# Twelve one-hot buffers instead of two in the three SAGE passes of a four-layer graph network

## The reference

```python
deg = segment_sum(ones, edge_dst); inv_deg = where(deg > 0, 1 / max(deg, 1), 0)
def sage_conv(h, Ws, Wn, b):
    agg = segment_sum(h[edge_src], edge_dst)
    return h @ Ws + (agg * inv_deg) @ Wn + b
h = relu(sage_conv(x, Ws0, Wn0, b0))    # 128 -> 256
h = relu(sage_conv(h, Ws1, Wn1, b1))    # 256 -> 256
h = relu(sage_conv(h, Ws2, Wn2, b2))    # 256 -> 128
```

## Time and profile before

| | us |
|---|---|
| median of three runs | 5223.72 (5216.58 to 5224.33) |
| the profiled execution | 5251.98 |
| its span, first to last instruction | 5250.2 |
| PE, DVE, ACT, POOL busy in it | 3245.7, 2924.6, 2771.9, 2886.8 |

### The profile page before, as it was taken

How to read it: one execution, slowest core, us unless ns; L and a number is a source line. 1 busy time by engine, 2 the same in 40 slices (tenths; PEclk the granted TensorE clock), 3 DMA queues, 4 the chain that set the end, 5 groups by cost and what they waited for, 6 DMA issues and landing times.

```text
span 5250.2 us, 70737 instructions
## 1 busy us (share of the span) xinstructions
PE 3245.7 (62%) x16464; PEld 2658.9 (51%) x16465; DVE 2924.6 (56%) x6078; ACT 2771.9 (53%) x5854; POOL 2886.8 (55%) x2818
## 2 busy tenths in 40 slices
PE   4666667778885778884233364555723335777776
PEld 3555554667774667673223244444522324655554
DVE  3666674999997999996000001112100003999997
ACT  1656664777774777773333333333323332777773
POOL 3455521666663666663666625666166662666661
PEclk7888888665555665555555577777855555999996
DMA  4344421223332323321111122333111111333331
GB/s 141 110 118 120 121 75 35 76 76 78 78 78 52 76 76 77 76 75 42 43 46 47 45 64 76 91 91 89 30 44 46 47 45 39 97 98 96 96 98 30
DMA packets 326787, 385.94 MB, mean 74 GB/s; under 512 B 68200, under 2 KB 267806, under 8 KB 326270
## 3 DMA queue, kind: packets, MB, share of 16 engines
q0 software_dynamic: 102496, 236.78, 16.2%
q1 hardware_dynamic: 221910, 142.28, 9.8%
q10 hardware_dynamic: 2218, 4.94, 0.3%
HBM read 366.52 MB, written 17.21 MB: 73 GB/s over the span
## 4 chain that ended last, share of the span: by engine, by line
PE 31%; another core or an unknown queue 21%; DVE 17%; issue 15%; ACT 11%; DVEq 3%; DMA 1%; SPq 1%; ACTq 0%; POOL 0%
PE ps L737 6%; ACT onehot L882 5%; DVE big L1166 4%; PE ps L595 4%; PE ps L686 3%; PE ps L724 3%; ACT onehot L888 2%; DVE w_run L1344 2%; DVE y_sb L1166 2%; PE ps L716 2%; PE ps L790 2%; PE ps L785 2%; PE ps L519 2%; DVE big L1369 2%
## 5 line engine op out<-in xcount | busy, mean ns | idle before, releaser
L476 POOL DMA_INDIRECT big<-table_sage,src_block x1173 | 1110.3, 947 | 852.5 <-issue 331.6
L462 POOL DMA_INDIRECT rows<-table_gat,src_idx x832 | 924.4, 1111 | 746.3 <-PE ps L659 278.5
L882 ACT ACTIVATE onehot<-iota,dst_rel 128x128 f32<-128x128 f32 x1664 | 530.6, 390 | 1400.5 <-remote 1031.4
L785 PE MATMUL ps<-big,onehot 128*128 x2496 | 536.1, 385 | 789.9 <-ACT onehot L888 459.9
L785 PEld LDWEIGHTS ps<-big,onehot 128*128 128x128 f32 x2496 | 476.2, 283 | 847.2 <-issue 842.5
L737 PE MATMUL ps<-y_sb,onehot 128*128 128x136 f32 (+2 forms) x2496 | 664.2, 425 | 81.5 <-DVE big L1166 73.5
L1537 DVE TENSOR_TENSOR y_sb<-ps,inv_row 128x512 f32<-128x512 f32 (+1 forms) x14 | 8.0, 645 | 1226.3 <-PE ps L785 1226.3
L462 POOL DMA_INDIRECT rows<-table_pool,src_idx x416 | 480.5, 1155 | 311.6 <-PE ps L663 119.6
L1166 DVE TENSOR_TENSOR big<-big,ps 128x257 f32 (+3 forms) x1664 | 576.2, 346 | 87.1 <-PE ps L737 24.9
L737 PEld LDWEIGHTS ps<-y_sb,onehot 128*128 128x128 f32 x2496 | 516.3, 278 | 143.9 <-DVE big L1166 118.0
L476 POOL DMA_INDIRECT big<-table_mlp,src_block x391 | 370.8, 948 | 344.0 <-DVE ps L1186 186.4
(11 more groups left out here) (231 smaller groups left out, 5925.4 us busy)
## 6 DMA issues: line engine op xcount, KB each, us to landing
ea_sb<-in_ea_blocks SPq DMA_DIRECT2D x832, 64.0 KB
big<-neg_rows SPq DMA_DIRECT2D x312, 128.0 KB
ea_sb<-rel_rows SPq DMA_DIRECT2D x208, 128.0 KB
big<-table_sage,src_block POOLq DMA_INDIRECT x1173
rows<-table_gat,src_idx POOLq DMA_INDIRECT x832
rows<-table_pool,src_idx POOLq DMA_INDIRECT x416
big<-table_mlp,src_block POOLq DMA_INDIRECT x391
w_sb<-in_wpack ACTq DMA_DIRECT2D x1, 2374.0 KB
```

The lines of the kernel that those rows point to most:

```text
L462: pool.indirect_dma_start(to[g % 2][:, j, 0:ROW[k]], None, table[k], bass.IndirectOffsetOnAxis(src_idx[:, step:step + 1], 0)).then_inc(loa ...
L476: pool.indirect_dma_start(ring[:, (block + RING_FIRST[k]) % (n * G), :], None, table[k], bass.IndirectOffsetOnAxis(src_block[:, block:bloc ...
L785: mm = pe.matmul(to, onehot[:, b, j, :], row(j, 0), start=False, stop=False, skip_group_check=True)
L882: ins = act.activation(onehot[:, b, j, :], iota[:, 0:P], ACT.Square, bias=values[:, bass.ds(x * G + j, 1)], scale=-1.0)
```

## The change

The three SAGE passes take their one-hots from twelve buffers in turn. The two buffers of before are kept; the other ten are cut out of tiles that have other uses in other passes: `rows` (four groups), `ea_sb` (two), `w_run` and `s_run` (two each). ACT's group g now waits until group g - 12 is summed. Since `s_run` is scratch for the ring's slot numbers before sage0, ACT also waits for `slots_ready` once, at group 10 of sage0. PE reads the same buffers in the same turn. Sizes, operations and counts are as before, and so are the queues of POOL, SP and DVE; the ring's size and POOL's own wait are not touched. The mlp, attention and pool passes keep two buffers.

```diff
+        def groups_in(tile, first=0):
+            words = tile.rearrange("p g f -> p (g f)") if len(tile.shape) == 3 else tile
+            return [words[:, at:at + G * P].rearrange("p (g e) -> p g e", g=G) for at in range(first, words.shape[1], G * P)]
+
+        sage_onehots = [buf for tile in (onehot, rows, ea_sb) for b in range(2) for buf in groups_in(tile[:, b])]
+        sage_onehots += [buf for tile in (w_run, s_run) for b in range(2) for buf in groups_in(tile[:, b, :])]
+
+        def onehot_of(k, g):
+            if k in SAGE:
+                return sage_onehots[g % len(sage_onehots)]
+            return onehot[:, g % 2]
...
-                        mm = pe.matmul(to, onehot[:, b, j, :], row(j, 0), start=False, stop=False, skip_group_check=True)
+                        mm = pe.matmul(to, onehot_of(k, g)[:, j, :], row(j, 0), start=False, stop=False, skip_group_check=True)
...
-                            mm = pe.matmul(ps[:, 7, j * P:(j + 1) * P], onehot[:, b, j, :], row(j, 1), start=True, stop=True)
+                            mm = pe.matmul(ps[:, 7, j * P:(j + 1) * P], onehot_of(k, g)[:, j, :], row(j, 1),
+                                           start=True, stop=True)
...
             def mark_pass(k):
                 for g in range(NG):
-                    square_distances(k, g, g % 2, dst_rel)
-                    mark_edges(k, g, g % 2)
+                    n = len(sage_onehots)
+                    if k == "sage0" and g == n - 2:
+                        act.wait_ge(slots_ready, 2)
+                    if g >= n:
+                        act.wait_ge(summed, base[k] + g - n + 1)
+                    for j in range(G):
+                        ins = act.activation(onehot_of(k, g)[:, j, :], iota[:, 0:P], ACT.Square,
+                                             bias=dst_rel[:, g * G + j:g * G + j + 1], scale=-1.0)
+                    ins.then_inc(squares_ready, 1)
+                    act.wait_ge(squares_ready, SQUARED.index(k) * NG + g + 1)
+                    act.activation(onehot_of(k, g), onehot_of(k, g), ACT.Relu, bias=ones[:, 0:1], scale=-1.0)\
+                       .then_inc(onehot_ready, 1)
```

## The result

The changed kernel takes 5191.69 us, median of five runs (5188.38 to 5195.11), against 5223.72 us for the kernel before beside it (5216.58 to 5224.81): a ratio of 0.9947 (95% interval 0.9936 to 0.9957), so 32 us less. The prediction was 71 us less. The direction is right, and the time lies in the range, but less than half of the forecast gain came.

The account below looks back on a forecast made before the run. Gathers were taken as each SAGE pass's floor, with late PE completions keeping passes above it. Gains of 57 + 14 + 0 = 71 us from 5223.7 gave 5153, predicted as 5150 us, range 5060 to 5235.

Parts of the forecast that it names:

- floor of the gathers: POOL in each SAGE pass: 391 gathers back to back take 489 us, the least time of a pass.
- the loop: SAGE passes: a late completion on PE makes the one-hot late, then the sum, then the freeing of the ring.
- late completion: PE's finished sums reach the other engines late, 12 and 29 us at the start of sage2.
- (1): ACT's side: same squares and relus, ten more buffers and one new wait on `slots_ready`, costed at nothing.
- (2): POOL's waits on `summed` in sage0 and sage2 fall from 72.5 to 44 us each, together 57 us gained.
- PE then follows the landings: With one-hots ready, PE sums a group some 5 us after its last gather was issued.
- what would show it: Expected signs: POOL's waits about 50 us, 11 or 12 pauses, PE's sums released by gathers, tails 17 us, sage1 within 10.
- the last link: End of the chain of delays in the SAGE passes: a late sum frees the ring late, so POOL waits.
- (3): Ends of sage0 and sage2 after the last gather: 16.8 us in place of 21.6 and 26.2, gain 14 us.
- (4): sage1: ACT isn't in the loop that sets the pace, so 0 us, with -10 to +95 us as ends.
- PE is really late, or POOL's window alone decides: Rival on the SAGE passes, 17%: the lead wins nothing except the tails at most, 5224 to 5210 us.
- "slower" rival: Rival, 13%: completions handed out one at a time while POOL gathers, each open group costing another pause; 5377 us.

Follow-up runs that it names:

- chip 0: Both kernels run again unchanged on another chip than the first experiments': kernel before 4734.56 us, changed kernel 4731.28 us, ratio 0.9989.

## Why the prediction was partly right

**What bounds the kernel.** The floor of the gathers was read rightly: where nothing disturbs it, a pass is 487 us of gathers, for 489 worked out. That POOL waits on `summed` was right too. The first link of the loop, "late completion", was right in kind: the reports are late, on ACT as on PE. It was wrong in size and form: the prediction took it for a lateness of at most 29 us, and it grows with every group that PE finishes in such a stretch.

**(1), no cost.** Right: ACT's busy time in the passes is 198, 203 and 198 us (203, 205 and 202 before), and no wait for `slots_ready` shows.

**(2), 57 us: the step that failed.** It rested on two sentences: a late `summed` is late by up to 29 us, of which POOL's window bears about 20; and "PE then follows the landings", a group being summed 5 us after its last gather was issued, with another group or two reported while POOL gathers. The first half of what would show it did come: PE's sums are released by gathers in place of ACT. Here are PE's waits in sage0, of the kernel before and then of the changed one:

```profile
PE ps L785 <- ACT onehot L888: 268.0, 46, 20.3
PE ps L785 <- issue: 111.3, 27, 19.6
```

```profile
PE ps L797 <- DMA big<-table_sage,src_block: 199.9, 67, 4.4
PE ps L797 <- issue: 136.2, 92, 3.4
```

But with ACT out of the loop PE runs ahead of its reports. Groups 2 and 3 of sage0 are reported 35 and 48 us late in place of at most 29, and then PE needs 36 us for groups 6 and 7. POOL's six groups of window run out in 30 us. The rows of before held the sign: the report of group 3 of sage2 is 17 us later than that of group 2, for one more group, and 29 us was where two buffers stopped PE from piling up more. The "issue" waits of PE, 111 us before and 136 us after, were there too.

POOL's runs did grow, from at most 20 gathers to mostly 24 to 28, near the 28 to 32 forecast, but the pauses between them grew too, from 3 to 4 us to 4 to 5. The term came out as 9 + 9 = 18 us. The runs with PE late on purpose show the last link alone: where a sum comes late, ACT's lead does nothing for POOL's waits.

**(3), the tails, 14 us.** Right: 7.4 + 8.8 = 16 us, at 14.2 and 17.4 in place of 16.8. In the later runs (chip 0), where PE isn't behind at the last gather, the tails go from 16.8 and 17.7 to 13.2 and 15.9 us.

**(4), sage1, 0.** Right within its 10 us, 619 to 615 us, but not because nothing changed in the loop: POOL paused some 2.0 us after every 8 gathers before, and in the changed kernel some 2.45 us after every 12. What came of it is 6 us less of waits.

**The rivals.** "PE is really late, or POOL's window alone decides" had 17% and 5210 us at the most. Its second half is nearest to what came: the waits kept most of their sum, and the window decides; its time was too high by 18 us. Its first half the trace doesn't bear out, as four reports came within 2.0 us. I put against it that group 3 began while group 2 was unreported; with two buffers never more than two groups are in PE, too few to tell. The Trainium skill, "Perfetto Trace Analysis", Tensor Engine Instruction, says that a matmul's end in the trace is an estimate. No run here shows such an end to be wrong: the 104 reports of sage0 on the later chip agree with the ends within 0.02 us, and the late ones of the first runs come in bursts that point at the report.

The "slower" rival (13%, 5377 us) had the mechanism, reports handed out one at a time while POOL gathers, about every 20 us, with several groups open when POOL stops. It didn't have the price: it let each open group cost a pause of its own, but some 8 us after POOL stops the held reports come all at once.

**What stays open.** Why reports took 1.4 us an instruction in the first runs and not in those on three chips later, with the same program and, on chip 0, gathers of the same length and the same clock in the pass. As the first runs' chip isn't known, a difference of chips and a state that passed can't be told apart. No later run met these late reports, so that they depend on gathers without a pause is seen in the first traces only, and whether a wider ring or shorter runs of gathers would help against them wasn't tried.

## What to carry to other kernels

When reports come late, ask whether the lateness is fixed or grows: set the distance between two releases (17 to 22 us here) beside the distance between the pieces of work (5 us). If it grows, a longer lead only makes the backlog longer, and a window sized for one late report runs out. Several reports at one moment (here four groups in 2.0 us, work for 6.3) tell that the work was done and the reports were held. More buffers ahead of a late engine buy only its catching up and its tail; its consumer's window is what bears the lateness (twelve buffers: nothing of 227 us of waits; a ring twice as long: three quarters). Run the kernel before on a second chip, or at another time, ahead of tuning a wait that no instruction in the trace explains: here 489 us, and most of what the change was to cure, were not there.

## What the hardware showed

Unexpected were the reports at 1.40 us for each instruction on PE and ACT in the same stretch, with ACT's own squares (four in 1.26 us) and POOL's gathers (1.25 us apart before, in and after the stretch) undisturbed; that the held reports came some 8 to 9 us after POOL's last gather (2505.76, and 2513.5 to 2515.3); and a difference of 10% between the first runs and all later ones (5224 and 4735 us) that lies mostly in the four passes that gather into a ring. POOL's idle time ahead of the gathers of the SAGE passes was 852.5 us and ahead of those of mlp, by the same page, 344.0; in the later run it was 594.4 and 166.2. These are 436 of the 516 us between the two profiled executions of the kernel before (5251.98 and 4736.27).
